# Scores and masks in four quarters of 32 keys: a change to the attention stage of a fused attention and FP4 layer

## The chip, the cores and the metric

One of the eight cores of a Trainium2 chip runs the whole program. Its engines work side by side, each through its own list of instructions: TensorE (PE, matrix products; its weight loads are listed as PEld), VectorE (DVE), ScalarE (ACT), GpSimd (POOL) and SyncE (SP, which issues DMAs). They wait for each other by semaphores. The metric is the device time of one execution in microseconds, as the median of several runs.

## The reference

A layer norm without parameters, then attention and a gated layer beside each other, both added to the input. Batch 4, 2048 tokens, width 256, 16 heads of 16 elements; the gated layer has 704 inner columns and quantises its inputs and weights to FP4 in blocks of 16.

```python
def reference(x, Wqkv, Wout, bout, w_gate, w_up, w_down):
    xn = _layernorm(x, axis=-1)
    # attention, causal, 16 heads of 16
    q, k, v = split_heads(xn @ Wqkv.T)
    dots = jnp.einsum('bhid,bhjd->bhij', q, k) * 16 ** -0.5
    dots = jnp.where(causal_mask, -jnp.inf, dots)
    out = jnp.einsum('bhij,bhjd->bhid', softmax(dots), v)
    attn = merge_heads(out) @ Wout.T + bout
    # gated layer: fp4_linear quantises both operands in blocks of 16
    h = silu(fp4_linear(xn, w_gate)) * fp4_linear(xn, w_up)
    return x + attn + fp4_linear(h, w_down)
```

## The kernel before

Four phases follow each other: the weights are quantised and turned (to some 70 us), q, k and v are computed as sums of bf16 parts, a shift phase finds for each query a maximum over its scores (tiles named m_S, m_DIFF), and the main phase, from 996 us on, computes attention and the gated layer together. The change touches the main phase alone.

The main phase runs a hardware loop over the 4 batches. In each, `attention_steps` makes 160 steps, written out one after another: 4 groups of 4 heads (hg), in each 4 chunks of 512 queries (c), in each the blocks of 128 keys up to the diagonal (j), so 4, 8, 12 or 16 steps a chunk. The last four blocks of a chunk are diagonal: only the queries from the block's first key on are computed (`st.skip`), so `st.width` is 512, 384, 256 and 128 columns there and 512 in all other steps. Of the 160 steps 64 are diagonal.

In a step TensorE does this, in order:

- S, the scores of the step (line 907), keys on the 128 output partitions, queries along the columns: one product for each of the 4 heads, weights from `k_st` (128 rows by 128 keys, bf16), moving operand `q_st`. Heads 0 and 1 (half 0) go to one pair of PSUM banks, `S[0]`, heads 2 and 3 to `S[1]`. At a diagonal step a second product adds the causal mask (line 910): the identity times `future`, a 128x128 tile with -1e30 where the key comes after the query, onto the first 128 columns. The last product of a half counts `scored[half]` up.
- O, the value products of the step before (line 923): for each of the 4 heads 32 output columns, namely 16 value columns, a column of ones for the softmax's sum, and zeros. Head s writes partitions 32s to 32s+31 of the bank `O`, so the four heads stand in four column tiles of the array. Both operands are fp32 and the hardware makes two passes of each product.
- F, a piece of the gated layer, in some steps. `GATED_AT` fixes by k, the step's number within a tile of 10 steps, what it is: the turning of x (k = 0, line 936, with the down products of two tiles ago, line 983, ahead of it), gate products (k = 2, 5) and up products (k = 3, 6) (line 943), turning of h (k = 8, 9, line 973). Steps k = 1, 4 and 7 have no such piece (`GATED_FIRST_AT` holds for the first tile, which has fewer). These products have 128 output columns.

ScalarE takes the exponential of each half, 128 by two heads by `st.width`, into `probs` (line 1052), when `scored[half]` has been counted, and does pieces of the gated layer between them. A half of S may be written again when its exponential is done (`exped[half]`, the wait at the head of `scores`); O waits for both exponentials of its step. VectorE normalises each chunk's O when its last step is done and runs the gated layer's elementwise chain with GpSimd. SP loads `q_st` for a chunk when the O of the chunk two before is free. After the 160 steps of a batch a flush follows: the remaining F pieces and the output projection (line 994).

Of the kernel before, what the change touches and what calls it, by code (L numbers as in the profile page):

```python
# [14 lines left out]
P = 128  # L15
# [20 lines left out]
SLOT = 32  # L36
QC = 512
# [744 lines left out]
GATED_FIRST_AT = {2: ("turn", 0), 4: ("gate", 0), 5: ("up", 0), 7: ("gate", 1), 8: ("up", 1)}  # L782


def gated_op(n, k):

    return (GATED_AT if n else GATED_FIRST_AT).get(k, (None, None))


def main_phase(nc, once, loop_sems, wts, ident, x_rows, bout, out_rows, dram):  # L790
# [13 lines left out]
    with ExitStack() as ctx:  # L804
        def sb(name, shape, dt=F32):
            return ctx.enter_context(nc.sbuf_tensor(name, shape, dt))

        def two(name, shape, dt=F32):
            return [sb(f"{name}{p}", shape, dt) for p in range(2)]

        def ps(name, shape):
            return ctx.enter_context(nc.psum_tensor(name, shape, F32))
# [5 lines left out]
        q_st, k_st = two("q_st", [P, HG, QC], BF16), two("k_st", [P, HG, T], BF16)  # L818
        ident_bf, future = sb("ident_bf", [P, P], BF16), sb("future", [P, P], BF16)
# [6 lines left out]
        S = [ps(f"S{h}", [P, 2, QC]) for h in range(2)]  # L826
# [72 lines left out]
        def _(pe):  # L899
            def scores(b, st, half):  # L900

                p = st.hg % 2
                pe.wait_ge(exped[half], b * nsteps + st.n + PRIMED)
                if st.n == 0:
                    pe.wait_ge(y_final, b * tiles + PRIMED)
                for s in (2 * half, 2 * half + 1):
                    ins = pe.matmul(S[half][:, s % 2, 0:st.width], k_st[p][:, s, st.j * P:(st.j + 1) * P],  # L907
                                    q_st[st.c % 2][:, s, st.skip:QC], start=True, stop=not st.diagonal)
                    if st.diagonal:
                        ins = pe.matmul(S[half][:, s % 2, 0:P], ident_bf[:, :], future[:, :], start=False, stop=True)  # L910
                ins.then_inc(scored[half], 1)

            def values(b, st):
# [85 lines left out]
            with pe.Fori(0, B) as b:  # L999
                for st in steps:  # L1000
                    n, k = divmod(st.n, per_tile)
                    op, ch = gated_op(n, k)
                    if st.c == 0 and st.first:
                        if st.hg < 2:
                            pe.wait_ge(k_ones[st.hg], 1)
                        pe.wait_ge(group_ld[st.hg % 2], b * (2 * 16 * group_dmas) + 16 * group_dmas * (st.hg // 2 + 1) + PRIMED)
                    if st.first:
                        pe.wait_ge(q_ld[st.c % 2], b * (chunks // 2 * 16 * q_dmas) + 16 * q_dmas * (st.chunk // 2 + 1) + PRIMED)
                    scores(b, st, 0)
                    scores(b, st, 1)  # L1010
                    if st.n:
                        values(b, steps[st.n - 1])
                    if k == 0 and n >= 2:
                        down(b, n - 2)
                    if op == "turn":
                        x_turn(b, n)
                    elif op == "gate":
                        gate(b, n, ch)
                    elif op == "up":
                        up(b, n, ch)  # L1020
                    elif k in (8, 9) and n >= 1:
                        h_turn(b, n - 1, k - 8)
# [11 lines left out]
        def _(act):  # L1034
# [34 lines left out]
            with act.Fori(0, B) as b:  # L1069
                for st in steps:  # L1070
                    n, k = divmod(st.n, per_tile)
                    op, ch = gated_op(n, k)
                    exps(b, st, 0)
                    exps(b, st, 1)
                    if op == "turn":
                        act.wait_ge(xt_ps, b * tiles + n + 1 + PRIMED)
                        act.activation(xt_hi[:, :], F[0][:, 0:KD * P], ACT.Copy).then_inc(xt_hi_done, 1)  # L1077
                    elif op == "gate":
                        gate_parts(b, n, ch)
                    elif k in (8, 9) and n >= 1:  # L1080
                        h_high(b, n - 1, k - 8)
                    if k == 9 and n + HEAD_TILES < tiles:
                        if n == 0:
                            act.wait_ge(y_st, b * (16 * (len(STORES) - 1)) + PRIMED)
                        load_tile(b, n + HEAD_TILES)
                for part in range(2):
                    h_high(b, tiles - 1, part)
                for first, last in STORES:
                    store(b, first, last)
# [303 lines left out]
```

## Time and profile before

| | us |
|---|---|
| median of 3 runs | 2762.43 |
| lowest and highest | 2761.91, 2763.21 |
| the profiled execution | 2762.52 |
| its span in the profile | 2760.8 |
| main phase in it | 1765, from 996 on |

The profile gives for every instruction its start and duration; a line L907 is line 907 of the kernel above. A product's duration counts from its start to the modelled end of its results, so that durations of consecutive products overlap: how fast TensorE works through its list is read from the distance between starts. "128\*32" behind MATMUL is rows by output columns of the weights, the form behind it the moving operand. In a row of the timeline, "x4" merges neighbours of one line and form that follow without a gap; its time is from the first one's start to the last one's end.

### The profile page before, as it was taken

How to read it: one execution, taken by the hardware profiler on the slowest of the kernel's cores; microseconds unless marked ns; L12 is line 12 of the kernel's file. 1: busy time of each engine (PE TensorE's matmuls, PEld its weight loads, DVE VectorE, ACT ScalarE, POOL GpSimd, SP SyncE). 2: the span in 40 equal slices, each digit the busy share in tenths (PEclk: the TensorE clock that was granted, in tenths of full speed). 3: DMA queues.
4: the chain of work that ended last, by engine and by line, in shares of the span. 5: the costliest groups of instructions: out<-in, count | busy, mean ns of one | idle time of the engine just before them, and what ended most of it. 6: DMA issues, size and time to landing. Idle time of an engine off the chain costs nothing.

```text
span 2760.8 us, 58289 instructions
## 1 busy us (share of the span) xinstructions
PE 2562.2 (93%) x18228; PEld 1304.5 (47%) x18228; DVE 1934.7 (70%) x5533; ACT 2038.4 (74%) x3502; POOL 722.6 (26%) x550
## 2 busy tenths in 40 slices
PE   2995999999999859999999999999999999999999
PEld 1883444444444424444454444444444445444455
DVE  7995999999999935655645656655656654566555
ACT  1554999999999847777758777775777775777775
POOL 3563334433333221122111112111121111212111
PEclk7997999999999979999999999999999999999999
DMA  2785555555445342202222112123022031220200
GB/s 70 238 272 123 75 75 75 76 72 71 71 70 72 45 84 38 51 19 39 47 78 48 32 31 46 29 58 80 22 42 43 21 76 50 40 47 23 41 24 32
DMA packets 118622, 175.70 MB, mean 64 GB/s; under 512 B 25648, under 2 KB 95024, under 8 KB 117808
## 3 DMA queue, kind: packets, MB, share of 16 engines
q1 hardware_dynamic: 97392, 147.33, 28.6%
q10 hardware_dynamic: 16576, 15.73, 2.1%
q0 software_dynamic: 4352, 8.92, 1.3%
q8 instruction: 153, 2.51, 0.4%
q14 instruction: 149, 1.22, 0.2%
HBM read 129.37 MB, written 42.53 MB: 62 GB/s over the span
## 4 chain that ended last, share of the span: by engine, by line
PE 54%; ACT 4%; issue 4%; SPq 1%; DMA 1%; DVE 0%; ACTq 0%; POOL 0%; DVEq 0%; POOLq 0%
PE O L923 17%; PE S L907 15%; PE F L943 10%; PE F L983 5%; ACT probs L1052 4%; PE F L973 2%; PE S L994 2%; PE S L910 2%; SPq L528 1%; PE F L936 1%; DMA y<-in_L_attn_x_dram 1%; DMA q_st<-s_shift 0%; DVE o_turned L1258 0%; ACTq L1047 0%; ACT xt_hi L1077 0%
## 5 line engine op out<-in xcount | busy, mean ns | idle before, releaser
L1052 ACT ACTIVATE probs<-S 128x1024 f32<-128x1024 f32 (+3 forms) x1280 | 1074.5, 897 | 227.6 <-PE S L910 84.1
L907 PE MATMUL S<-q_st,k_st 128*128 128x512 bf16 (+3 forms) x2560 | 648.8, 351 | 75.0 <-DMA q_st<-s_shift 38.4
L730 ACT ACTIVATE m_excess<-m_DIFF 128x512 f32<-128x512 f32 (+7 forms) x1536 | 647.1, 472 | 88.3 <-PE m_DIFF L690 42.3
L748 DVE CUSTOM_DVE_ANT_0 m_excess<-m_S,m_excess 128x512 f32<-128x512 f32 (+7 forms) x1536 | 700.7, 530 | 11.7 <-PE m_S L690 9.2
L923 PE MATMUL O<-probs,v_sb 128*32 128x512 f32 (+3 forms) x5120 | 603.6, 543 | 2.2 <-POOL v_sb L1129 2.2
L688 PE MATMUL m_S<-m_k,m_q 128*128 128x512 bf16 (+7 forms) x1536 | 483.1, 325 | 26.7 <-DVE m_row_max L748 17.3
L688 PE MATMUL m_DIFF<-m_k,m_q_diff 128*128 128x512 bf16 (+7 forms) x1536 | 478.0, 319 | 29.5 <-DMA m_q_diff<-s_q 29.2
L907 PEld LDWEIGHTS S<-q_st,k_st 128*128 128x128 bf16 x2560 | 213.7, 98 | 418.2 <-ACT probs L1052 235.1
L632 POOL TENSOR_TENSOR m_q_diff<-m_zero,m_q 48x4096 bf16<-48x4096 bf16 x32 | 224.4, 7011 | 429.0 <-DMA m_q<-s_q 418.3
L688 PEld LDWEIGHTS m_S<-m_k,m_q 128*128 128x128 bf16 x1536 | 148.3, 97 | 275.8 <-DVE m_row_max L748 194.9
L1246 DVE TENSOR_TENSOR ht_lo<-F,ht_hi 128x512 fp32r<-128x512 f32 (+1 forms) x128 | 71.0, 557 | 232.5 <-ACT ht_hi L1067 232.5
L1112 POOL TENSOR_TENSOR h_norm<-gated,h_rscale 128x704 f32<-128x704 f32 x64 | 88.8, 1388 | 441.5 <-DVE h_rscale L1188 441.5
L923 PEld LDWEIGHTS O<-probs,v_sb 128*32 128x32 f32 x5120 | 100.9, 108 | 212.3 <-issue 205.1
L690 PE MATMUL m_S<-m_future,m_ident 128*128 128x64 bf16 x1024 | 197.2, 193 | 0.0
L690 PE MATMUL m_DIFF<-m_future,m_ident 128*128 128x64 bf16 x1024 | 196.6, 193 | 0.0
L910 PE MATMUL S<-future,ident_bf 128*128 128x128 bf16 x1024 | 195.6, 221 | 0.0
L1097 POOL TENSOR_TENSOR x_norm<-xn,x_rscale 128x256 f32<-128x256 f32 x64 | 48.2, 753 | 553.0 <-DVE x_rscale L1188 553.0
L1221 DVE TENSOR_SCALAR tanh<-tanh 128x352 int32<-128x352 int32 x128 | 72.4, 565 | 164.0 <-ACT decay L1062 164.0
L688 PEld LDWEIGHTS m_DIFF<-m_k,m_q_diff 128*128 128x128 bf16 x1536 | 150.9, 98 | 73.4 <-issue 31.0
L1252 DVE TENSOR_TENSOR y<-F,y 128x256 f32<-128x256 f32 x64 | 27.1, 424 | 175.9 <-PE F L983 175.9
L1059 ACT ACTIVATE decay<-F 128x352 f32<-128x352 f32 x128 | 59.3, 463 | 107.7 <-PE F L943 107.7
L1118 POOL TENSOR_TENSOR h_fp<-h_norm,h_scale 128x704 f32<-128x704 f32 x64 | 88.8, 1387 | 191.1 <-DVE h_norm L1198 191.1
(163 smaller groups left out, 4189.8 us busy)
## 6 DMA issues: line engine op xcount, KB each, us to landing
k_st<-s_k SPq DMA_DIRECT2D x96, 256.0 KB, 8.6
q_st<-s_q SPq DMA_DIRECT2D x384, 64.0 KB
s_q<-a_part SPq DMA_DIRECT2D x48, 256.0 KB, 3.0
s_k<-a_part SPq DMA_DIRECT2D x48, 256.0 KB, 2.2
m_q<-s_q SPq DMA_DIRECT2D x96, 128.0 KB, 3.8
m_k<-s_k SPq DMA_DIRECT2D x96, 128.0 KB, 6.7
m_q_diff<-s_q SPq DMA_DIRECT2D x96, 128.0 KB, 8.1
m_k<-s_k SPq DMA_DIRECT2D x96, 124.0 KB, 5.2
```

The source lines that it names most:

```text
L632: pool.tensor_tensor(q_diff[p][rows, :, :], zero[rows, 0:1].unsqueeze(2).to_broadcast([MAX_ROWS, MAX_LOAD, T]), q_st[p][rows, :, :], ALU.s ...
L688: ins = pe.matmul(out[:, 0:keys], q[:, h % MAX_LOAD, i * P:(i + 1) * P], of, start=True, stop=mask is None)
L690: ins = pe.matmul(out[:, keys - PAIR:keys], ident_bf[:, :], mask, start=False, stop=True)
L730: act.activation(excess[u % MAX_EXCESS][:, 0:keys // 2], DIFF[u % MAX_BUFS][:, 0:keys // 2], ACT.Relu) \
L748: dve.tensor_tensor_reduce(larger, S[u % MAX_BUFS][:, 0:keys // 2], larger, 1.0, -3e38, ALU.add, ALU.max, column).then_inc(reduced[u % MAX ...
L907: ins = pe.matmul(S[half][:, s % 2, 0:st.width], k_st[p][:, s, st.j * P:(st.j + 1) * P], q_st[st.c % 2][:, s, st.skip:QC], start=True, sto ...
L910: ins = pe.matmul(S[half][:, s % 2, 0:P], ident_bf[:, :], future[:, :], start=False, stop=True)
L923: ins = pe.matmul(o[s * SLOT:(s + 1) * SLOT, st.skip:QC], v_sb[st.hg % 2][:, st.j, s * SLOT:(s + 1) * SLOT], probs[s // 2][st.n % 2][:, s ...
L943: ins = pe.matmul(F[f][:, 0:ICH], m[:, kk * P:(kk + 1) * P], w[:, kk, ch * ICH:(ch + 1) * ICH], start=k == 0, stop=k == len(terms) - 1)
L983: ins = pe.matmul(F[1][:, 0:D], h[:, m * P:(m + 1) * P], w[:, m, :], start=k == 0, stop=k == len(terms) - 1)
L1052: act.activation(probs[half][st.n % 2][:, :, 0:st.width], S[half][:, :, 0:st.width], ACT.Exp, scale=SCALE).then_inc(exped[half], 1)
L1112: pool.tensor_tensor(fp4_blocks(h_norm[:, :]), fp4_blocks(gated[n % 2][:, :]), per_block(h_rscale[:, :], hb), ALU.mult).then_inc(h_normed, 1)
```

## The change

The score product of a head is written as four products, each of 32 keys: quarter a takes the weights of keys 32a to 32a+31 and writes partitions 32a to 32a+31, with all `st.width` queries as moving operand. The mask of a diagonal step is written as four products too, quarter a on the columns 0 to 32(a+1)-1, beyond which its keys don't need a mask in this block. The waits and the counting of `scored` stay as they were; the count is on the last quarter.

```diff
+def quarters():
+
+    return [slice(a * SLOT, (a + 1) * SLOT) for a in range(P // SLOT)]
+
+
...
                 for s in (2 * half, 2 * half + 1):
-                    ins = pe.matmul(S[half][:, s % 2, 0:st.width], k_st[p][:, s, st.j * P:(st.j + 1) * P],
-                                    q_st[st.c % 2][:, s, st.skip:QC], start=True, stop=not st.diagonal)
+                    for at in quarters():
+                        ins = pe.matmul(S[half][at, s % 2, 0:st.width], k_st[p][:, s, st.j * P + at.start:st.j * P + at.stop],
+                                        q_st[st.c % 2][:, s, st.skip:QC], start=True, stop=not st.diagonal)
                     if st.diagonal:
-                        ins = pe.matmul(S[half][:, s % 2, 0:P], ident_bf[:, :], future[:, :], start=False, stop=True)
+                        for at in quarters():
+                            ins = pe.matmul(S[half][at, s % 2, 0:at.stop], ident_bf[:, at], future[:, 0:at.stop],
+                                            start=False, stop=True)
                 ins.then_inc(scored[half], 1)
```

TensorE's list before, around a step without a piece of the gated layer (L903 is the head of a step's scores, sizes are output columns of the array by moving columns):

```order
L943 MATMUL F<-w_up_hi,xt_lo 128x352
L903 REGISTER_ALU
L907 MATMUL S<-q_st,k_st 128x512 x4
L923 MATMUL O<-probs_0,v_sb 32x512 x4
L903 REGISTER_ALU
L907 MATMUL S<-q_st,k_st 128x512 x4
L923 MATMUL O<-probs_1,v_sb 32x512 x4
```

The same place in the changed program, where line 913 has the scores, 931 the value products and 951 the gate and up products:

```order
L951 MATMUL F<-w_up_hi,xt_hi 128x352
L951 MATMUL F<-w_up_lo,xt_hi 128x352
L951 MATMUL F<-w_up_hi,xt_lo 128x352
L908 REGISTER_ALU
L913 MATMUL S<-q_st,k_st 32x512 x16
L931 MATMUL O<-probs_1,v_sb 32x512 x4
L908 REGISTER_ALU
L913 MATMUL S<-q_st,k_st 32x512 x16
L931 MATMUL O<-probs_0,v_sb 32x512 x4
```

The order is the same; from the first S on all products up to the next F have 32 output columns, and there are four times as many of S.

A diagonal step before, width 128, with the value products of the step ahead of it:

```order
L907 MATMUL S<-q_st,k_st 128x128
L910 MATMUL S<-future,ident_bf 128x128
L907 MATMUL S<-q_st,k_st 128x128
L910 MATMUL S<-future,ident_bf 128x128
L907 MATMUL S<-q_st,k_st 128x128
L910 MATMUL S<-future,ident_bf 128x128
L923 MATMUL O<-probs_0,v_sb 32x256 x4
```

And a diagonal step in the changed program, width 384, from its third head on, where line 917 has the masks:

```order
L917 MATMUL S<-future,ident_bf 32x128
L913 MATMUL S<-q_st,k_st 32x384 x4
L917 MATMUL S<-future,ident_bf 32x32
L917 MATMUL S<-future,ident_bf 32x64
L917 MATMUL S<-future,ident_bf 32x96
L917 MATMUL S<-future,ident_bf 32x128
L931 MATMUL O<-probs_0,v_sb 32x512 x4
L908 REGISTER_ALU
```

Each head's product and its mask have become four and four, the mask's with 32, 64, 96 and 128 columns. TensorE's list of the whole program has 7,934 rows where it had 7,166 (equal neighbours are merged in a row); the lists of the other engines hold the same instructions in the same order.

## Rows read from the trace of the kernel before

**Rows 1.** The page: busy share of each engine; the chain, by engine, by line.
```profile
PE 2562.2 (93%) x18228; PEld 1304.5 (47%) x18228; DVE 1934.7 (70%) x5533; ACT 2038.4 (74%) x3502; POOL 722.6 (26%) x550
PE 54%; ACT 4%; issue 4%; SPq 1%; DMA 1%; DVE 0%; ACTq 0%; POOL 0%; DVEq 0%; POOLq 0%
PE O L923 17%; PE S L907 15%; PE F L943 10%; PE F L983 5%; ACT probs L1052 4%; PE F L973 2%; PE S L994 2%; PE S L910 2%; SPq L528 1%; PE F L936 1%; DMA y<-in_L_attn_x_dram 1%; DMA q_st<-s_shift 0%; DVE o_turned L1258 0%; ACTq L1047 0%; ACT xt_hi L1077 0%
```

**Rows 2.** Busy time by stretch, main phase: busy us (count), granted clock, DMA share.
```profile
core 0: us, PE busy (x) PEld busy (x) DVE busy (x) ACT busy (x) POOL busy (x), PEclk, DMA share, GB/s
996.00:2761.00 1765.00, 1715.50 (x12160) 835.66 (x12160) 1027.05 (x2144) 1288.89 (x1856) 328.80 (x336) 0.99 0.21 43
```

**Rows 3.** The page's groups: count, busy us, mean ns, idle before and its releaser.
```profile
L907 PE MATMUL S<-q_st,k_st 128*128 128x512 bf16 (+3 forms) x2560 | 648.8, 351 | 75.0 <-DMA q_st<-s_shift 38.4
...
L923 PE MATMUL O<-probs,v_sb 128*32 128x512 f32 (+3 forms) x5120 | 603.6, 543 | 2.2 <-POOL v_sb L1129 2.2
...
L910 PE MATMUL S<-future,ident_bf 128*128 128x128 bf16 x1024 | 195.6, 221 | 0.0
```

**Rows 4.** Timeline of TensorE, full-width step: start us, length us (L923 without start: durations).
```profile
1508.06 0.32 PE L943 MATMUL F<-w_up_lo,xt_hi 128*128 128x352 f32 x1
1508.22 0.32 PE L943 MATMUL F<-w_up_hi,xt_lo 128*128 128x352 f32 x1
...
1508.38 1.04 PE L907 MATMUL S<-q_st,k_st 128*128 128x512 bf16 x4
...
1508.83 0.38 PE L907 MATMUL S<-q_st,k_st 128*128 128x512 bf16 x1
...
1509.04 0.38 PE L907 MATMUL S<-q_st,k_st 128*128 128x512 bf16 x1
1509.35 0.64 PE L923 MATMUL O<-probs,v_sb 128*32 128x512 f32 x4
...
L923 PE MATMUL O<-probs,v_sb x4: 617/617/617, 1509.3 to 1509.4; 128*32 128x512 f32 x4
...
1509.80 0.61 PE L923 MATMUL O<-probs,v_sb 128*32 128x512 f32 x4
...
1510.35 0.39 PE L907 MATMUL S<-q_st,k_st 128*128 128x512 bf16 x1
```

**Rows 5.** Timeline of TensorE, value products of 384 and 128 columns, both passes.
```profile
1569.20 0.53 PE L923 MATMUL O<-probs,v_sb 128*32 128x384 f32 x4
...
1569.54 0.51 PE L923 MATMUL O<-probs,v_sb 128*32 128x384 f32 x4
...
1501.08 0.32 PE L923 MATMUL O<-probs,v_sb 128*32 128x128 f32 x4
...
1501.21 0.29 PE L923 MATMUL O<-probs,v_sb 128*32 128x128 f32 x4
```

**Rows 6.** Timeline of TensorE, the end of a diagonal step's scores of width 512.
```profile
1564.30 0.22 PE L910 MATMUL S<-future,ident_bf 128*128 128x128 bf16 x1
1564.35 0.38 PE L907 MATMUL S<-q_st,k_st 128*128 128x512 bf16 x1
1564.57 0.22 PE L910 MATMUL S<-future,ident_bf 128*128 128x128 bf16 x1
1564.72 0.62 PE L923 MATMUL O<-probs,v_sb 128*32 128x512 f32 x2
```

**Rows 7.** Timeline of weight loads and products, value products, and F after them.
```profile
1509.35 0.16 PEld L923 LDWEIGHTS O<-probs,v_sb 128*32 128x32 f32 x8 [0.42 <-issue]
...
1504.28 0.19 PEld L943 LDWEIGHTS F<-w_gate_hi,xt_hi 128*128 128x128 f32 x1 [0.84 <-issue]
1504.28 0.43 PE L943 MATMUL F<-w_gate_hi,xt_hi 128*128 128x352 f32 x1
1504.38 0.19 PEld L943 LDWEIGHTS F<-w_gate_lo,xt_hi 128*128 128x128 f32 x1
...
1504.54 0.32 PE L943 MATMUL F<-w_gate_lo,xt_hi 128*128 128x352 f32 x1
...
1504.70 0.32 PE L943 MATMUL F<-w_gate_hi,xt_lo 128*128 128x352 f32 x1
```

**Rows 8.** Timeline of a step without F, then two rows of the waits.
```profile
1509.03 1.02 ACT L1052 ACTIVATE probs<-S 128x1024 f32<-128x1024 f32 x1 [0.45 <-PE S L907]
...
1509.03 1.94 ACT L1052 ACTIVATE probs<-S 128x1024 f32<-128x1024 f32 x2 [0.45 <-PE S L907]
...
1511.02 0.60 PE L907 MATMUL S<-q_st,k_st 128*128 128x512 bf16 x2
1511.56 1.06 PE L923 MATMUL O<-probs,v_sb 128*32 128x512 f32 x8
...
PEld S L907 <- ACT probs L1052: 235.1, 340, 3.0
...
PE S L907 <- ACT probs L1052: 25.9, 61, 2.7
```

## The prediction

> **What bounds the kernel now.** I read the busy shares and the chain of the page first [rows 1]. TensorE is busy in 93% of the span and the chain that ended last runs through it for 54%, with the value products (O), the score products (S) and the gated layer's products (F) ahead of ScalarE's exponentials at 4%. The attention stage is the last 1,765 us [rows 2]: TensorE busy for 1,715, ScalarE for 1,289, granted clock 0.99, the 2.4 GHz level. So TensorE sets its pace, and what counts there is not the modelled busy time but the distance from one product's start to the next one's. Second, the page's groups [rows 3] give the counts: 2,560 score products, 1,024 masks, 640 steps. Third, I read starts in the timeline.
>
> A full-width score product of 512 columns starts 0.21 to 0.22 us before the next [rows 4], that is 512 columns at 2.4 GHz (213 ns) and some 3 ns. A mask of 128 columns takes 0.05 to 0.06 [rows 6], 53 ns and 3. The value products run as four of 32 output columns side by side: four start within 20 ns (a group of 0.64 us, 617 ns for one), so 7 ns apart, and their second pass starts 0.45 us after the first, where 512 columns in two cycles each are 427 ns [rows 4]. The excess is 25 to 27 ns, and it is the same at 384 columns (1569.20 to 1569.54: 0.34 to 0.35 for 320) and at 128 (1501.08 to 1501.21: 0.13 for 107) [rows 5]. It is four spacings of 6.7 ns: a group's first member seems to start only when the last member of the group before has streamed.
>
> **Price of a change of form.** From the last score product to the first value product 0.31 us pass (1509.04 to 1509.35) where 0.216 would do, and from mask to value product 0.15 (1564.57 to 1564.72) where 0.056 would [rows 4, 6]: 93 ns. The way back costs as much: second pass at 1509.80, its last member 20 ns later, the next score product at 1510.35, so 0.53 against 0.43 [rows 4]. From F, which has the scores' 128x128 form, to S nothing is lost: 0.16 as between two F products [rows 4].
>
> **The change part by part.**
>
> Score products. One product of 216 ns becomes a group of four quarters. In the value products' manner a group takes 213 + 27 = 240 ns. The extra 24 ns times 2,560 is **+61.7 us**, less at no width, as the excess didn't depend on it.
>
> Masks. One of 56 ns becomes four of 32, 64, 96 and 128 columns. The last is still 128 wide, so the group takes 53 + 27 = 80 ns: 24 ns times 1,024 is **+24.7 us**. The shorter triangles save nothing, because the widest member goes last.
>
> Changes of form. Each step is S, O of the step before, then F in 110 of the 160 steps of a batch. Now S to O and O to F (or to the next S) both change: with the flush, 320 in a batch. After it S and O share a form; what is left is O to F (110), F to S (109), and three around the flush: 222. So 98 x 4 = 392 go, at 93 ns **-36.5 us**. For the value of the new F to S change I take the nearest row, S to O. The bounds: nothing, as F to S now, would be 436 x 93 = 41 us less; a change as O to F shows it, where the first F product is followed after 0.26 us instead of 0.16 [rows 7], would be 436 x 0.107 = 47 us more.
>
> Where the saving can't arrive. A step without F loses both its changes, 186 ns, but these steps wait for ScalarE already. In the stretch of rows 8 the second half of S starts at 1511.02 where TensorE was ready at 1510.35 + 0.44 = 1510.79; the exponential it waits for ran from 1509.95 to 1510.97 (two in 1.94 us from 1509.03), behind the one from 1509.03, which began when the first two score products of 1508.38 had ended. This chain from 1508.38 to 1511.02 (2.64 us) holds none of the removed changes. From the end of F to the first O after it, 1508.38 to 1511.56, 3.18 us pass before. After: 0.093 (F to S) + 2.64 + 0.044 (a second quarter group starts 24 ns later and its last member 20) + 0.48 (two groups, then O with no change) = 3.26, or 0.08 more. The sum of the first three terms gives this stretch 4 x 24 x 2 - 93 x 2 = +6 ns plus 11 for the start after O, say 0.02. So 0.065 us is to be added for each such pair; the program has 31 full-width ones in a batch, 124 in all: **+8 us**. The exposed waits of S for the exponentials, 235 + 26 us of idle time by the waits [rows 8], most of it under a running product, say the same: ScalarE is close behind TensorE here.
>
> Added instructions: 16 loads and 16 products a step for scores where 4 and 4 were, and at diagonal steps as many again. The narrowest diagonal step has 64 in 4 x (80 + 80) = 640 ns, 10 ns each. Eight weight loads of the value products stand within 0.16 us at 109 ns each [rows 7], 7 ns apart, four of them in pairs with products; TensorE's issue keeps up, as far as a burst shows it. Cost zero, with the long products before as cover; without it some narrow steps would grow. DVE, GpSimd and the DMA queues get the same instructions in the same order.
>
> Weight loads. Four loads of 32 columns replace one of 128. Loads of a 128-column F operand follow each other by 0.10 us [rows 7], 27 ns for 32 columns. If the four quarters had to share one path, a group could not be shorter than 107 ns. This touches the groups of 80 ns only: 1,024 masks and 256 score groups of width 128, so 1,280 x 27 = 35 us. The value products' loads 7 ns apart [rows 7] speak against it, and I take zero. The Trainium skill, TensorEngine Tiling (Array Packing), Restrictions, says that column tiling disables the fast weight load; by it the quarters would lose the quick load that a full bf16 operand has, and this is the case of the 35 us, a sum of 93. No row here shows a bf16 load in a 32-column form.
>
> Sum: 61.7 + 24.7 - 36.5 + 8 = **+58 us**. On the profiled span of 2,760.8 that is 2,818.8, with the 1.7 us around it (that run: 2,762.5) 2,820.5; the median of the runs, 2,762.4, lies 0.1 below that run: **2,820 us**.
>
> **Rivals.**
>
> *Quarters overlap across groups* (faster). If the excess of 27 ns belongs to the two passes of an fp32 product and not to the form, the groups follow as closely as full products. Then both plus terms vanish, -36.5 stays, and in 124 steps ScalarE's chain takes the 0.186 back (23 us): -13 at best, some less in the narrow steps: -10, 2,752 us. It decides at the group's excess over a full product: at 10 / 3,584 = 3 ns or less the change pays, at 24 it doesn't. For it: a bf16 product has one pass. Against: the excess is exactly four times the members' spacing at three widths.
>
> *A smaller spacing*. If members started 4 ns apart, a group would have 16 ns over its streaming, 13 over a full product: 3,584 x 0.0133 = 48 - 36.5 + 8 = +19, 2,782 us. The Trainium skill, TensorE: Matmul & The Clock Gate, Measured speedup vs the span model, gives about 4 ns per tile; the rows here show 6.7, and the measurement decides.
>
> *Loads share a path*: +93, 2,855 us, as worked out above.
>
> *No overlap at all* (the change doesn't do what it says). If quarters of the scores ran one after another, a product would take 4 x 220 = 880 ns: 0.66 x 2,560 = 1.7 ms more, about 4,500 us. The value products in the same column tiles, which overlap fully, speak against it; that they read 4 bytes in two cycles, the quarters 2 bytes in each, is the same rate.
>
> **How the numbers follow.** Forecast 2,820: 0.60, with its own range from 2,820 - 41 to 2,820 + 47, that is 2,779 to 2,867. Loads share a path 0.15; smaller spacing 0.08; overlap across groups 0.13; no overlap 0.04. The range 2,779 to 2,868 takes in all but the last two, 0.17 left out. A measurement tells 0.2%, 5.5 us, from no change. Faster by more comes from overlap across groups, nearly whole: 0.11; within 0.2%: 0.03, its rest and the low end; slower: 0.86.
>
> **What would show it.** Quarter groups of 512 columns start 0.24 us apart, masks 0.08 before the next; the last score quarter is followed by O after 0.22 and not 0.31; F is followed by S after 0.25 and not 0.16; O is followed by S in steps without F with no added 0.09, yet the second half of S still waits for the exponential. Wrong it would be if groups follow after 0.22 or less, if mask groups take over 0.1, or if F to S costs nothing or twice as much.

## The result and the profile after

| | before | after |
|---|---|---|
| median us (4 runs each) | 2762.82 | 2745.04 |
| lowest and highest | 2761.91, 2766.09 | 2744.02, 2746.34 |
| ratio to before, 95% interval | | 0.9934 (0.9917 to 0.9951) |
| profiled execution, its span | 2762.52, 2760.8 | 2744.02, 2742.3 |

The change makes the kernel faster by 18 us, 0.7%. The prediction said 2,820 us, slower, with 0.86 on slower: wrong in direction, and the time lies below its whole range of 2,779 to 2,868 us. On the page of the changed kernel line 913 has the scores, 917 the masks, 931 the value products, 1060 the exponentials and 951 the gate and up products. Three rows of the page and one row of busy time by stretch:

```profile
PE 2513.9 (92%) x28980; PEld 1370.3 (50%) x28980; DVE 1935.2 (71%) x5533; ACT 2031.9 (74%) x3502; POOL 723.5 (26%) x550
...
L913 PE MATMUL S<-q_st,k_st 128*32 128x512 bf16 (+3 forms) x10240 | 671.4, 352 | 102.0 <-ACT probs L1060 56.4
...
L917 PE MATMUL S<-future,ident_bf 128*32 128x32 bf16 (+3 forms) x4096 | 218.0, 201 | 0.2
...
998.00:2742.00 1744.00, 1668.02 (x22912) 902.08 (x22912) 1027.78 (x2144) 1282.04 (x1856) 329.37 (x336) 0.99 0.22 44
```

TensorE has 10,752 more products and is busy for less time; the main phase went from 1,765 us [rows 2] to 1,744. Its idle time ahead of S that ScalarE ended grew from 25.9 us [rows 8] to 56.4. By stretches, each from the last product of one piece of the gated layer to the first of the next, the two traces differ by 19 us: 10.4 stand in stretches of two steps of which at least one is diagonal, 7.8 in stretches of one step, and only 0.9 in the 112 stretches of two full-width steps.

The timeline of TensorE around a full-width step with no piece of the gated layer, which answers to [rows 4, 8] (start us, length us; a row of x4 is one group of quarters, or one pass of the value products):

```profile
1502.62 0.32 PE L951 MATMUL F<-w_up_lo,xt_hi 128*128 128x352 f32 x1
1502.78 0.32 PE L951 MATMUL F<-w_up_hi,xt_lo 128*128 128x352 f32 x1
...
1503.03 0.40 PE L913 MATMUL S<-q_st,k_st 128*32 128x512 bf16 x4
...
1503.26 0.39 PE L913 MATMUL S<-q_st,k_st 128*32 128x512 bf16 x4
...
1503.47 0.39 PE L913 MATMUL S<-q_st,k_st 128*32 128x512 bf16 x4
...
1503.69 0.39 PE L913 MATMUL S<-q_st,k_st 128*32 128x512 bf16 x4
...
1503.90 0.60 PE L931 MATMUL O<-probs,v_sb 128*32 128x512 f32 x4
...
1504.33 0.60 PE L931 MATMUL O<-probs,v_sb 128*32 128x512 f32 x4
...
1504.77 0.40 PE L913 MATMUL S<-q_st,k_st 128*32 128x512 bf16 x4
...
1505.00 0.39 PE L913 MATMUL S<-q_st,k_st 128*32 128x512 bf16 x4
...
1505.69 0.40 PE L913 MATMUL S<-q_st,k_st 128*32 128x512 bf16 x4 [0.30 <-ACT probs L1060]
...
1506.13 1.03 PE L931 MATMUL O<-probs,v_sb 128*32 128x512 f32 x8
1507.09 0.66 PE L981 MATMUL F<-ident,h_fp 128*128 128x128 f32 x4
```

Read the starts. F to S takes 0.25 us where it took 0.16: the new change of form, at the forecast price. Groups of quarters follow each other after 0.21 to 0.23 us, as whole products did [rows 4], and not after 0.24. The value products follow without a change of form: the last group of scores begins at 1503.69 and O at 1503.90, so 0.22 us where 0.31 passed before. O's second pass comes after 0.43 (1503.90 to 1504.33), where before it came after 0.45 [rows 4]; over all full-width steps the median went from 453 to 429 ns, and at 128 columns from 133 to 109. This last saving the prediction had no place for. From 1504.77 on ScalarE sets the pace, as before: the second half of S could start at 1505.22, one group's 0.216 after 1505.00, and starts at 1505.69, when an exponential has ended.

### The profile page after: what moved, and what is told of

Its sections match the earlier page's. It is cut to its first block, busy times and chain, and to the rows that moved or that the text cites. A ratio compares the mean times of both kernels' runs of the same rounds, so it can differ in the third digit from the quotient of the medians.

```text
span 2742.3 us, 79793 instructions
## 1 busy us (share of the span) xinstructions
PE 2513.9 (92%) x28980; PEld 1370.3 (50%) x28980; DVE 1935.2 (71%) x5533; ACT 2031.9 (74%) x3502; POOL 723.5 (26%) x550
## 4 chain that ended last, share of the span: by engine, by line
PE 52%; ACT 5%; issue 4%; DMA 1%; SPq 1%; DVE 0%; ACTq 0%; POOL 0%; DVEq 0%; POOLq 0%
PE S L913 16%; PE O L931 14%; PE F L951 10%; PE F L991 5%; ACT probs L1060 5%; PE F L981 2%; PE S L1002 2%; PE S L917 2%; SPq L528 1%; DMA y<-in_L_attn_x_dram 1%; PE F L944 1%; DMA q_st<-s_shift 0%; DVE o_turned L1266 0%; ACTq L1055 0%; ACT xt_hi L1085 0%
## 5 line engine op out<-in xcount | busy, mean ns | idle before, releaser
L1060 ACT ACTIVATE probs<-S 128x1024 f32<-128x1024 f32 (+3 forms) x1280 | 1065.7, 899 | 219.4 <-PE S L913 83.9
L913 PE MATMUL S<-q_st,k_st 128*32 128x512 bf16 (+3 forms) x10240 | 671.4, 352 | 102.0 <-ACT probs L1060 56.4
L913 PEld LDWEIGHTS S<-q_st,k_st 128*32 128x32 bf16 x10240 | 242.6, 95 | 457.2 <-ACT probs L1060 250.8
L917 PE MATMUL S<-future,ident_bf 128*32 128x32 bf16 (+3 forms) x4096 | 218.0, 201 | 0.2
L931 PEld LDWEIGHTS O<-probs,v_sb 128*32 128x32 f32 x5120 | 157.0, 111 | 84.0 <-issue 2.3
L917 PEld LDWEIGHTS S<-future,ident_bf 128*32 128x32 bf16 x4096 | 145.0, 97 | 3.4 <-issue 2.8
```

Of the source, the lines that this page charges most:

```text
L913: ins = pe.matmul(S[half][at, s % 2, 0:st.width], k_st[p][:, s, st.j * P + at.start:st.j * P + at.stop], q_st[st.c % 2][:, s, st.skip:QC], ...
L917: ins = pe.matmul(S[half][at, s % 2, 0:at.stop], ident_bf[:, at], future[:, 0:at.stop], start=False, stop=True)
L931: ins = pe.matmul(o[s * SLOT:(s + 1) * SLOT, st.skip:QC], v_sb[st.hg % 2][:, st.j, s * SLOT:(s + 1) * SLOT], probs[s // 2][st.n % 2][:, s ...
L1060: act.activation(probs[half][st.n % 2][:, :, 0:st.width], S[half][:, :, 0:st.width], ACT.Exp, scale=SCALE).then_inc(exped[half], 1)
```

## The experiments

The kernel before was measured beside every group of runs, with medians from 2,762.7 to 2,763.6 us. The two theories are that of the prediction, called the group theory (a group of quarters costs 24 ns more than a whole product), and what the trace of the changed kernel suggests, called the entry theory: those 24 ns belong to the change of form ahead of the value products, and ScalarE takes back a part of what the missing changes save.

**Value products twice.** On the kernel before:

```diff
-                for s in range(HG):
-                    ins = pe.matmul(...)
+                for again in range(2):
+                    for s in range(HG):
+                        ins = pe.matmul(..., start=st.first and not again, stop=st.last and again == 1)
```

> The kernel before with every step's value products written twice, so four passes of four members stand in a row where two stood (numerator and the softmax's sum both double, the output keeps its value). Entry theory: the 24 to 27 ns that the second pass comes late belong to the change of form ahead of the block, so the second group starts 0.453 us after the first and the third and fourth 0.429 after the one before. Group theory (the recorded prediction's): 0.453 each time. The time grows by 640 steps of two more passes, 467 us of streaming, less some 30 to 50 of waits for ScalarE that vanish: about 3,190 by the first, 3,220 by the second.

The time was 3,198 us, one run, and the two theories' totals, 3,190 and 3,220, are too near to their own uncertainty to decide by. The starts do. TensorE's timeline of one block of four passes, line 924 here; a row that begins at a pass merges what runs on from it:

```profile
1683.30 1.06 PE L924 MATMUL O<-probs,v_sb 128*32 128x512 f32 x8
...
1683.76 1.04 PE L924 MATMUL O<-probs,v_sb 128*32 128x512 f32 x8
...
1684.19 1.04 PE L924 MATMUL O<-probs,v_sb 128*32 128x512 f32 x8
...
1684.62 0.61 PE L924 MATMUL O<-probs,v_sb 128*32 128x512 f32 x4
```

The second pass comes after 0.45 us, the third and fourth after 0.43 each. Over all 448 full-width blocks the medians are 453, 429 and 429 ns; at 384 columns 347, 323 and 322, at 256 240, 216 and 216, at 128 133, 109 and 109. The 24 ns are paid once, at the block's start. It isn't the step from bf16 to fp32 operands that costs them either: in the changed kernel that step is still there, without the change of form, and the second pass comes after 429 ns. Every block of the kernel before was entered by a change of form and had only two passes, so it had no distance between passes but the first after a change. Its durations held a hint, though: at all three widths of [rows 4, 5] the first pass is listed as 0.02 to 0.03 us longer than the second (0.64 and 0.61, 0.53 and 0.51, 0.32 and 0.29).

**Halved exponentials, before and after.** Each exponential takes one of its two heads; the kernel leaves out the other half of the work, so its output isn't the reference's. Not shown in the diff: `probs` is filled with ones once, and the engines wait for that.

```diff
-                act.activation(probs[half][st.n % 2][:, :, 0:st.width], S[half][:, :, 0:st.width], ACT.Exp,
+                act.activation(probs[half][st.n % 2][:, 0:1, 0:st.width], S[half][:, 0:1, 0:st.width], ACT.Exp,
...
```

> The kernel before, where each exponential takes only the first of its two heads; the other half of probs keeps ones. ScalarE is then far ahead of TensorE in every step. Both theories: the waits of S for the exponentials go, some 40 us, about 2,720. It is the base for the next run.

> The changed kernel with the same halved exponentials. Theory that ScalarE takes back a good part of what TensorE wins: without it the change is worth what the forms cost, 640 x 0.114 (S to O with the late second pass) + 196 x 0.09 (O to S) - 440 x 0.09 (F to S now) = 51 us, so about 2,670. Theory that ScalarE gives nothing back: the difference to the half-exp kernel of before stays at 18 us, about 2,702.

Measured: 2,714.2 us before (0.9822, 0.9805 to 0.9838) and 2,674.7 after (0.9679, 0.9663 to 0.9695). With ScalarE out of the way the change is worth 39.5 us, not 18: ScalarE takes back some 22.

The entry theory's 51 us was too much by 11. The two traces show two places. In the 28 stretches of two full-width steps at a chunk's start, where the theory has 6.4 us saved, 3.1 were lost: 12 of them took clearly longer than the rest, where 8 did in the kernel before, and in one of the 12 TensorE was idle for 0.77 us until the load of `q_st` had landed. And in six places TensorE stopped for 0.9 to 1.5 us, 7.2 us in all, at a moment when the profile shows nothing that it waited for (more on such stops below); away from the batches' starts the kernel before with halved exponentials has none of these. The other stretches saved more than the theory said, 0.284 us where it had 0.228 in the kind that follows.

Where the 22 go is shown by one kind of stretch, from the last product of a piece to the first of the next with two full-width steps between them. Timeline with halved exponentials, kernel before (lines 944 and 974 are pieces, 908 S, 924 O):

```profile
1496.44 0.32 PE L944 MATMUL F<-w_up_hi,xt_lo 128*128 128x352 f32 x1
...
1498.57 1.04 PE L908 MATMUL S<-q_st,k_st 128*128 128x512 bf16 x4
...
1500.54 0.66 PE L974 MATMUL F<-ident,h_fp 128*128 128x128 f32 x4
```

and the same kind of stretch in the changed kernel with halved exponentials (952 pieces, 914 S, 932 O):

```profile
1501.42 0.32 PE L952 MATMUL F<-w_up_hi,xt_lo 128*128 128x352 f32 x1
1501.66 1.05 PE L914 MATMUL S<-q_st,k_st 128*32 128x512 bf16 x16
1502.54 1.03 PE L932 MATMUL O<-probs,v_sb 128*32 128x512 f32 x8
1503.40 1.04 PE L914 MATMUL S<-q_st,k_st 128*32 128x512 bf16 x16
1504.26 1.03 PE L932 MATMUL O<-probs,v_sb 128*32 128x512 f32 x8
1505.22 0.43 PE L952 MATMUL F<-w_gate_hi,xt_hi 128*128 128x352 f32 x1
```

4.10 us against 3.80; over 84 stretches of this kind the medians are 4.094 and 3.810, 0.284 saved in each. In the full kernels the same stretches took 4.334 and 4.316, 0.018 saved: for before 1508.22 [rows 4] to 1512.55, for after 1502.78 to 1507.09 above. ScalarE's chain eats 0.27 of 0.28 us, 84 times, which is the 22 us (in the other stretches its effects, +4 and -3 us, nearly cancel). Stretches with one full-width step don't wait for it: 2.121 to 2.088, and 2.121 to 2.087 with halved exponentials.

**Masks all 128 wide.**

```diff
-                            ins = pe.matmul(S[half][at, s % 2, 0:at.stop], ident_bf[:, at], future[:, 0:at.stop],
+                            ins = pe.matmul(S[half][at, s % 2, 0:P], ident_bf[:, at], future[:, :],
...
```

> The changed kernel with all four mask quarters 128 columns wide instead of 32, 64, 96 and 128. Theory that the gain comes from the form alone: the last quarter is as wide as before, so nothing changes, 2,745 within 3 us. Rival, that column tiles with short masks run ahead and so start the value products early: without the short triangles this is lost, up to the whole gain, 2,755 to 2,763.

2,747.3 us, 0.9939 (0.9923 to 0.9956), the ratio of the changed kernel within its interval. The short triangles bring nothing that the runs can tell from noise. The column tiles do run ahead of each other, as a diagonal step of the narrowest width in the trace of after shows:

```profile
1492.63 0.24 PE L913 MATMUL S<-q_st,k_st 128*32 128x128 bf16 x4
...
1492.97 0.40 PE L931 MATMUL O<-probs,v_sb 128*32 128x256 f32 x2
1492.99 0.22 PE L913 MATMUL S<-q_st,k_st 128*32 128x128 bf16 x1
1493.00 0.26 PE L917 MATMUL S<-future,ident_bf 128*32 128x96 bf16 x2
1493.04 0.65 PE L931 MATMUL O<-probs,v_sb 128*32 128x256 f32 x6
```

Value products of two tiles start at 1492.97, while score and mask quarters of the other tiles still come. But the step ends with its last tile, whose mask is 128 wide, so this wins little: with wide masks the stretches of two narrow steps took 0.015 to 0.02 us more, 3 us over the whole trace, and all others, the batches' starts apart, the same. All 32 score and mask products of the step above started within 0.41 us.

**Two halves of 64 keys.**

```diff
-    return [slice(a * SLOT, (a + 1) * SLOT) for a in range(P // SLOT)]
+    return [slice(a * PAIR, (a + 1) * PAIR) for a in range(P // PAIR)]
```

> The changed kernel with scores and masks in two halves of 64 keys instead of four quarters of 32. Theory that the gain needs the very form of the value products: S to O costs a change again, and F to S costs one that the kernel before didn't have, 440 x 0.09 = 40 us: about 2,790 to 2,802. Rival, that any smaller form will do (loads or tiles overlap better): at or below 2,750.

2,816.6 us, 1.0192 (1.0175 to 1.0209): 72 us above the quarters and 54 above before. The timeline from a piece through S to O, with 64 output columns:

```profile
1602.58 0.32 PE L951 MATMUL F<-w_up_hi,xt_lo 128*128 128x352 f32 x1
1602.83 1.05 PE L913 MATMUL S<-q_st,k_st 128*64 128x512 bf16 x8
...
1603.51 0.38 PE L913 MATMUL S<-q_st,k_st 128*64 128x512 bf16 x2
...
1603.82 0.64 PE L931 MATMUL O<-probs,v_sb 128*32 128x512 f32 x4
```

F to S costs the change (0.25) and S to O costs it too (0.31): 64 columns and 32 columns are different forms to the array. The gain of the quarters is not that they are small; it is that they have the form of the products behind them. The time is 15 to 27 us above what I had expected. Most of that is the price of the new change, taken at 0.09 us: a stretch of one full-width step took 2.233 us where it took 2.121 before, 0.112 more, one of two 0.124 more, and all 443 stretches together 52 us more, not 40. A part of it is that behind F to S the second group of halves comes 14 ns late too (240 ns).

**Masks whole between quarters.**

```diff
-                        for at in quarters():
-                            ins = pe.matmul(S[half][at, s % 2, 0:at.stop], ident_bf[:, at], future[:, 0:at.stop],
-                                            start=False, stop=True)
+                        ins = pe.matmul(S[half][:, s % 2, 0:P], ident_bf[:, :], future[:, :], start=False, stop=True)
```

> The changed kernel with the masks written whole, 128x128, as before, between scores in quarters. If each change between the forms costs some 0.09 to 0.11 us, a diagonal step has eight of them (into and out of each of four masks) where the changed kernel has none: 256 x 8 x 0.1 = 205 us, less what waits for ScalarE hide: 2,900 to 2,950. If a change costs only where fp32 operands are loaded, nothing: 2,745.

2,956.2 us, one run: 211 us above the changed kernel, for 205 expected from the changes alone, and 6 above the range of 2,900 to 2,950, which counted on waits to hide a part. Over the 2,048 added changes it is 0.103 us each. Scores (913) and masks (916) of one diagonal step:

```profile
1601.57 0.24 PE L913 MATMUL S<-q_st,k_st 128*32 128x128 bf16 x4
1601.74 0.23 PE L916 MATMUL S<-future,ident_bf 128*128 128x128 bf16 x1
1601.90 0.24 PE L913 MATMUL S<-q_st,k_st 128*32 128x128 bf16 x4
1602.07 0.23 PE L916 MATMUL S<-future,ident_bf 128*128 128x128 bf16 x1
```

Each starts 0.16 to 0.17 us after the one before, where 0.056 is the streaming: a change of form costs 0.10 to 0.12 us between bf16 operands too, in both directions.

**First half whole after a piece.** If ScalarE's chain decides, the place of the change of form matters, not the number only. In the steps behind a piece heads 0 and 1 stay whole, so that the change stands behind them (`has_piece(m)` tells whether a piece follows step m):

```diff
+                whole = half == 0 and st.n and has_piece(st.n - 1)
                 for s in (2 * half, 2 * half + 1):
+                    if whole:
+                        ins = pe.matmul(S[half][:, s % 2, 0:st.width], k_st[p][:, s, st.j * P:(st.j + 1) * P], ...)
+                        if st.diagonal:
+                            ins = pe.matmul(S[half][:, s % 2, 0:P], ident_bf[:, :], future[:, :], start=False, stop=True)
+                        continue
```

> The changed kernel, but in steps that follow a piece of the gated layer the scores of heads 0 and 1 (with masks) stay in the 128x128 form and the quarters begin with head 2. The number of changes is the same, the one from F to S is moved behind the first half. Theory that ScalarE's chain bounds many steps: the first exponential starts 0.09 us earlier in 440 steps, in those that wait for it the step ends earlier: 10 to 25 us less, 2,720 to 2,735. Rival, that only TensorE's sum counts: 2,745 within 3 us.

2,730.1 us, 0.9877 (0.9860 to 0.9893): 33 us below before and 15 below the changed kernel, with the same number of changes; the two intervals don't touch. The stretches of two full-width steps went from 4.316 to 4.203 us, those of one from 2.088 to 2.105.

The same order with halved exponentials (output not the reference's, as above):

> The run with the first half whole after a piece of the gated layer, with the halved exponentials. In the full computation that order was 15 us faster than the quarters throughout. Theory that this comes from ScalarE's chain alone (its first exponential starts 0.09 us earlier): with the halved exponentials there is nothing to gain, and the time is that of the quarters with halved exponentials, 2,675, or up to 5 above (one-step stretches took 16 ns more each). Rival, that TensorE itself loses less with the change of form behind the first half: again 10 to 15 us less, 2,660 to 2,665.

2,674.2 us, 0.9678 (0.9662 to 0.9695), against 0.9679 for quarters throughout with halved exponentials. The 15 us vanish with ScalarE's load. The gain is ScalarE's chain beginning earlier. TensorE's own sum is, if anything, worse: stretches of two full-width steps took 3.820 us against 3.810, those of one 2.104 against 2.087, and what evens this out is that the six stops of the quarters with halved exponentials don't occur here.

**Down products a step later.** On the changed kernel, with VectorE's addition moved likewise:

```diff
-                    if k == 0 and n >= 2:
+                    if k == 1 and n >= 2:
                         down(b, n - 2)
...
```

> The changed kernel with the down products (18 products, some 2.1 us) moved from step 0 of a tile to step 1, which had no piece of the gated layer, and with them VectorE's addition. Theory that steps without a piece wait for ScalarE while step 0 is long: step 1 waits no more and step 0 isn't idle, up to 15 us less, against two more changes of form in 56 steps, 56 x 0.2 = 11 us more: 2,735 to 2,750. If waits were unimportant: 2,756.

2,767.2 us, 1.0019 (1.0009 to 1.0028), 22 above the changed kernel: a miss, beyond the 11 us of two more changes in 56 steps. The theory of the waits gained nothing: TensorE's idle time ahead of S that ScalarE ended hardly shrank (54.6 us where it was 56.4), while ScalarE now waits longer for TensorE, as two rows of the waits of this kernel show:

```profile
ACT probs L1060 <- PE S L917: 156.5, 86, 37.3
...
ACT probs L1060 <- PE S L913: 140.8, 144, 2.9
```

In the changed kernel they were 74.5 and 83.9. The other 11 us come from elsewhere. In each batch TensorE stopped in the middle of a step's scores or value products, with nothing in the profile that it waited for ("issue"), for instance here:

```profile
1159.34 0.35 PE L913 MATMUL S<-q_st,k_st 128*32 128x384 bf16 x4 [2.67 <-issue]
```

There are seven such stops of 1.2 to 2.7 us, 14.0 us in all, that the changed kernel's trace doesn't have; after the one above the granted clock was 0.51, the 1.2 GHz level, for 3.4 us. Each ended some 3 us after the start of a transfer on the DMA queue that the page calls `q8 instruction`. That queue made 237 transfers in the changed kernel where it made 153 before, 84 more of 16 KB for the 21,504 added products and weight loads. That TensorE's own list of instructions came too late there is my reading; no run separates it from other causes.

**Next step's first scores ahead of the piece.** On the changed kernel, then with ScalarE's list in the same order, then TensorE's part on the kernel before (`loaded` holds the waits for a chunk's operands, which stood ahead of the scores):

```diff
...
-                    scores(b, st, 0)
...
+                    if st.first:
+                        loaded(st)
+                        scores(b, st, 0)
                     scores(b, st, 1)
                     if st.n:
                         values(b, steps[st.n - 1])
+                    if not st.last:
+                        scores(b, steps[st.n + 1], 0)
```

> The changed kernel with the scores of heads 0 and 1 of the next step written ahead of the piece of the gated layer instead of behind it (not across a chunk's start). The number of changes of form stays. Theory that ScalarE, idle or late behind a piece, is what holds the steps without a piece: it finds its next exponential ready while the piece runs, and much of the some 20 us that the halved exponentials uncovered comes, with the first quarter form's start hidden: 2,700 to 2,730. Rival, that ScalarE is simply full in these stretches (two exponentials of 0.93 us and a gate piece of 1.4 us): 2,740 to 2,750.

> As the run before, and ScalarE takes the next step's first exponential ahead of its own part of the piece too. Theory that the order of ScalarE's list matters where a gate piece comes: 5 to 15 us below the run before. Rival: the gate's part comes later, VectorE's chain with it, and the gate products wait: above it.

> The same reordering in the kernel before, scores and masks whole. There each step has two more changes of form at about 0.1 us where the next scores stand between value products and piece (value products to scores, and the change into the piece is saved): with a piece the number stays at two, so it should gain about what the changed kernel gains from it, 2,725 to 2,750. If the order only pays together with the quarters, 2,760 or more.

2,889.0 us (1.0442, 1.0403 to 1.0480), 2,755.9 (0.9970, 0.9958 to 0.9983) and 2,851.0 (1.0317, 1.0299 to 1.0334). All three miss: the first and the last were to be gains and are losses, and the second lies 133 us below the first, not 5 to 15. The trace of the first shows the main reason. TensorE and ScalarE behind a gate piece:

```profile
1605.94 1.03 PE L931 MATMUL O<-probs,v_sb 128*32 128x512 f32 x8
1607.77 0.61 PE L913 MATMUL S<-q_st,k_st 128*32 128x512 bf16 x8 [0.80 <-ACT probs L1066]
1608.32 0.43 PE L951 MATMUL F<-w_up_hi,xt_hi 128*128 128x352 f32 x1
...
1605.60 0.46 ACT L1073 ACTIVATE decay<-F 128x352 f32<-128x352 f32 x1 [1.32 <-PE F L951]
1605.96 0.46 ACT L1074 ACTIVATE tanh<-F 128x352 f32<-128x352 f32 x1
1606.31 0.50 ACT L1076 ACTIVATE decay<-decay 128x352 f32<-128x352 f32 x1
1606.69 1.94 ACT L1066 ACTIVATE probs<-S 128x1024 f32<-128x1024 f32 x2
```

ScalarE does its part of the gate piece first and reaches the exponential at 1606.69; the scores that overwrite its bank wait for it to end, 1607.77, and the next piece, which needs nothing of it, is queued behind them. TensorE's idle time ahead of S that ScalarE ended was 143.6 us here, 87 more than in the changed kernel, and 122.6 in the last run, 97 more than before. With ScalarE's list reordered it falls to 42.8, and the time comes back to 11 above the changed kernel, 8 below the kernel before. I had priced where the scores were needed and not what they themselves wait for.

The remaining 11 us don't show that the order is no gain. The trace of this second run has ten stops of the kind met in the run before, of 1.0 to 3.6 us, 23 us in all, and the first has five, 15.7 us in all; the kernel before in this order, with its shorter list, has none away from the batches' starts. What the order would be worth without them no run shows.

## Why the prediction was wrong, point by point

**The step that failed** is the reading of the value products' second pass, the term "a group takes 213 + 27 = 240 ns" and with it +61.7 us for score products and +24.7 us for masks. Both terms measured nothing: groups of 512 columns follow after 216 ns in the trace of the changed kernel, and the passes of doubled value products after 429 once the first is past. The rows were right (453 ns, and the same excess at every width), and I took it for a rule of the form. It was a constant price of the form's change, seen once per block because every block began with one. The four spacings of 6.7 ns matched by coincidence: in the doubled products the members still start 7 ns apart and the groups follow without excess.

**The rival that came near** was "quarters overlap across groups", with a chance of 0.13 and 2,752 us, 7 above the measured time. Its outcome held, its reason didn't: the excess doesn't belong to the two passes of an fp32 product, since the doubled fp32 products lose it after the first distance. It lacked the 24 ns that each of 640 blocks saves. Its 23 us for ScalarE, 124 steps at 0.186, agree with the measured 22 by luck: it was 84 stretches at 0.266.

**The price of a change** was right where it was 93 ns, and short by the 24 ns that I had booked as a group's cost. S to O therefore costs some 117 ns up to where O's second pass would be, and the new F to S 0.09 as taken. For a stretch of one full-width step: +94 (F to S), -93 (S to O), -24 (second pass) and -11 at O's end give -34, where -33 was measured. That the prediction's -36.5 for all changes lies near the 39.5 of the halved exponentials is luck as well: with the 24 ns the term is some -52, and some 12 of it were lost where the section on halved exponentials says.

**Where the saving can't arrive.** Mechanism and place were right: steps without a piece wait for ScalarE, and the saving there is lost. The size, +8 us, was too small because it was counted against a sum in which the groups' excess had used most of the saving up.

**Costs taken at nothing.** The sharing of a path by the weight loads didn't show: in the narrowest steps the scores and masks of the last tile still start 56 ns apart, where 107 would be needed, so the rival of 2,855 us fell. The added instructions cost nothing that shows in the changed kernel itself: 32 score and mask products of the narrowest step started within 0.41 us, and outside a batch's start its trace has no stop over 0.7 us of the kind described above. But in four of its variants such stops took 7 to 23 us, so zero is no rule. "No overlap at all" didn't occur.

**The range** left out the rival that came near. The rule of the Trainium skill that I had set aside by rows, about 4 ns for each tile (TensorE: Matmul & The Clock Gate, Measured speedup vs the span model), was nearer than the rows' 6.7: the four of 1503.03 take 0.40 us together and one of them 390 ns, so they start some 3 ns apart, and in the changed kernel the value products of 1503.90 do too (0.60 together, 592 ns for one). Neither figure enters the distance between groups, so both sums made of it were wrong. The other rule of the Trainium skill, that column tiling disables the fast weight load (TensorEngine Tiling (Array Packing), Restrictions), had no price here that a run shows.

## What to carry to other kernels

A constant excess at several widths tells that something is paid once per occurrence, but not what it is paid for: look for rows in which the suspected cause is there and the other is not, and if the trace has none, put real chance on the other reading. Products that stand next to each other on TensorE should have one tile form, the same one and not only a smaller one; where a change of form must stay, put it behind the products that another engine waits for. Before an operation is moved ahead, ask what it waits for and what is queued behind it. And when a variant misses, look for stops with no releaser in its trace before the order of work is blamed.

## What the runs showed of the hardware

A change between the 128x128 form and 32-column tiles cost 0.09 to 0.12 us in every pair seen, bf16 or fp32, in both directions, and so did one between 64-column and 32-column tiles. On top of it the second pass of fp32 value products entered by a change came 24 ns late, the second group of 64-column bf16 products 14 ns, that of 32-column bf16 products not at all (227 ns, as 226 between the first two whole products before). Column tiles of 32 advance on their own: in the narrowest diagonal steps one tile's value products start 0.07 us before another tile's last mask. Four bf16 products side by side stream 512 columns each in the 216 ns of one whole product. With 237 transfers on the instruction queue instead of 153, TensorE stopped in the middle of a batch for 0.9 to 3.6 us without a shown releaser in the traces of four variants of the changed kernel; that the one causes the other isn't shown.
